# Two graph layers on one core: moving the feature loads and stores to the Scalar engine's queue, reordering the first three chunks and splitting the last row's work

## The reference

```python
# layer 1
x_norm = layernorm(x, g_in, b_in)
logits = x_norm @ Wn + bn
gumbel = -log(-log(clip(u, EPS, 1)) + EPS)
y = hard(softmax(logits + gumbel)) + y_soft - y_soft     # straight-through
gate = y[:, 1]                                           # one number per node
view2 = (adj * gate[:, None] * gate[None, :]) @ x_norm
g = sigmoid(concat([x_norm, view2]) @ Wg + bg)
x1 = layernorm(x + layernorm(g * (x_norm @ W1 + b1) + (1 - g) * (view2 @ W2 + b2) + x, g_out, b_out))
# layer 2, on the Poincare ball: xt is the tangent image of x1 @ weight.T with the bias added
s = adj @ xt
h = proj(expmap0(proj(expmap0(s))), relu in the tangent space)   # norms, tanh, artanh per row
out = layernorm(x1 + h)
```

## Time and profile before

| | |
|---|---|
| median of three runs | 991.94 us |
| the three runs | 991.94, 4496.1, 988.4 us |
| profiled execution | 988.93 us |
| its span, first to last instruction | 987.1 us |
| mean granted clock of TensorE | 0.981 |

### The profile page before, as it was taken

The page is one execution under the profiler, slowest core; times in us unless marked ns, Lnnn a source line. Parts: engine busy times, 40 slices in busy tenths (PEclk is TensorE's granted clock), DMA queues, the critical chain, the costliest instruction groups (busy, mean ns, idle before and its releaser), DMA issues.

```text
span 987.1 us, 12612 instructions
## 1 busy us (share of the span) xinstructions
PE 914.8 (93%) x4052; PEld 725.5 (73%) x4052; DVE 798.6 (81%) x1778; ACT 692.0 (70%) x1233; POOL 225.5 (23%) x201
## 2 busy tenths in 40 slices
PE   3897998999999999999999999998999988989992
PEld 2554776877787777888888888886778766768772
DVE  3567898988898889788685867769999986988984
ACT  4685686868676656856564664576988977887883
POOL 2220211111111111101110100102003627264562
PEclk8999999999999999999999999999999999999997
DMA  6888696876868586958584565757899988999970
GB/s 241 288 305 305 228 423 265 317 297 256 321 233 341 212 327 232 335 214 298 206 304 169 210 253 185 259 204 261 328 355 410 368 342 332 355 390 353 357 314 21
DMA packets 51681, 281.72 MB, mean 285 GB/s; under 512 B 6512, under 2 KB 8224, under 8 KB 20512
## 3 DMA queue, kind: packets, MB, share of 16 engines
q1 hardware_dynamic: 49888, 277.78, 75.1%
q10 hardware_dynamic: 1728, 3.15, 0.8%
HBM read 271.44 MB, written 9.46 MB: 285 GB/s over the span
## 4 chain that ended last, share of the span: by engine, by line
PE 48%; DVE 22%; POOL 12%; ACT 7%; issue 4%; DMA 4%; SPq 2%; POOLq 0%; DVEq 0%; ACTq 0%
PE PS L986 14%; PE PS L988 14%; PE PS L987 13%; DVE AL L741 6%; DVE XGL L741 4%; DVE XTL L741 2%; POOL SINV L485 2%; DVE BS L690 2%; PE PS L1075 2%; PE PS L1071 2%; DMA A<-in_adjT_dram 2%; POOL e_rc L492 1%; POOL r_rs L462 1%; PE PS L984 1%; DMA xnt_scratch<-XNT 1%
## 5 line engine op out<-in xcount | busy, mean ns | idle before, releaser
L741 DVE TENSOR_TENSOR AL<-A,AH 128x1024 fp32r<-128x1024 f32 x251 | 299.6, 1220 | 42.9 <-ACT AH L559 41.9
L559 ACT ACTIVATE AH<-A 128x1024 fp32r<-128x1024 f32 x251 | 256.3, 1057 | 103.2 <-PE PS L988 84.3
L741 DVE TENSOR_TENSOR XGL<-A,XGH 128x1024 fp32r<-128x1024 f32 x119 | 139.4, 1217 | 9.0 <-ACT XGH L559 8.8
L986 PE MATMUL PS<-AH,XGH 128*128 128x512 f32 x344 | 137.5, 400 | 5.6 <-DVE AL L741 5.6
L988 PE MATMUL PS<-AH,XGL 128*128 128x512 f32 x344 | 134.4, 391 | 0.0
L987 PE MATMUL PS<-AL,XGH 128*128 128x512 f32 x344 | 134.3, 390 | 0.0
L986 PE MATMUL PS<-AH,XTH 128*128 128x512 f32 x298 | 118.5, 398 | 6.4 <-DVE AL L741 6.3
L559 ACT ACTIVATE XGH<-A 128x1024 fp32r<-128x1024 f32 x119 | 117.8, 1054 | 2.1 <-DMA A<-in_adjT_dram 2.1
L987 PE MATMUL PS<-AL,XTH 128*128 128x512 f32 x298 | 117.4, 394 | 0.0
L988 PE MATMUL PS<-AH,XTL 128*128 128x512 f32 x298 | 117.3, 394 | 0.0
L741 DVE TENSOR_TENSOR XTL<-A,XTH 128x1024 fp32r<-128x1024 f32 x92 | 109.7, 1220 | 5.1 <-ACT XTH L559 4.7
(11 more groups left out here) (236 smaller groups left out, 1558.4 us busy)
## 6 DMA issues: line engine op xcount, KB each, us to landing
A<-in_adjT_dram SPq DMA_DIRECT2D x243, 1024.0 KB, 6.8
XR<-in_x_dram SPq DMA_DIRECT2D x16, 256.0 KB, 4.8
GB<-gate_scratch SPq DMA_DIRECT2D x12, 256.0 KB, 3.7
XNT<-xnt_scratch SPq DMA_DIRECT2D x12, 256.0 KB, 4.1
x_scratch<-X SPq DMA_DIRECT2D x12, 256.0 KB, 7.7
xnt_scratch<-XNT SPq DMA_DIRECT2D x6, 256.0 KB, 3.4
xnt_scratch<-X1T SPq DMA_DIRECT2D x6, 256.0 KB, 3.7
FU<-in_x_dram SPq DMA_DIRECT2D x4, 256.0 KB, 3.9
```

Of the source, the lines that this page charges most:

```text
L559: a.activation(high(m), A[:, n % RING, h * HW:(h + 1) * HW], ACT.Copy).then_inc(S["hi"], 1)
L741: v.tensor_tensor(low(m), A[:, n % RING, h * HW:(h + 1) * HW], high(m).bitcast(F32), ALU.subtract).then_inc(S["lo"], 1)
L986: p.matmul(acc, hi[:, st], high(m)[:, mv], start=start, stop=False)
```

## The change

1. **Queues.** `load_x` and `store_xnt` move from SP's stream to ACT's. ACT's stream begins with `load_x(0)` to `load_x(2)`; later loads stand behind `normalize`, stores behind `gated`. SP starts with U and BNB, then the norm vectors and A's first tile, and issues the A tiles in a plain loop.
2. **The first three chunks.** On DVE `stats_pre(0)` goes ahead of the first operation on U, `neg_mean_pre(0)` ahead of the second, and `gate_end(0)` ahead of `neg_mean_pre(2)`. On ACT each logarithm stands around `normalize(0)`, `transposed(0)` goes ahead of `normalize(1)`, an exponential of one column (JUNK) is added ahead of `store_xnt(0)`, and `normalize(2)` stands behind `gated(0)`. TensorE does `rows_and_logits(0)` ahead of `transposes(1)`.
3. **The last row** (o = 11). ACT leaves out the four squares ahead of the relu, and DVE gets those sums from `bn_stats` as 128 * (mean^2 + variance). POOL's power of eight columns becomes two of four, the relu's half first. The final scaling and shifting is done by ACT for the left half and DVE for the right, and each half has a store of its own.
4. **All rows:** the places of `norm` and `store` in ACT's order go from 21 and 22 to 22 and 23.

```diff
...
 DVE_SECOND = {"take": 3, "floor": 7, "norms": 11, "add": 15, "mean": 18}
-ACT_SECOND = {"relu": 7, "tanh": 14, "norm": 21, "store": 22}
+ACT_SECOND = {"relu": 7, "tanh": 14, "norm": 22, "store": 23}
 PE_SECOND = {"turn": 2}
...
         def _(sp):
-            def load_x(k):
-                if k >= 3:
-                    sp.wait_ge(S["pre_y"], k - 2)
-                sp.dma_start(XIN[k % 3][:, :], x[k * P:(k + 1) * P, :]).then_inc(S[f"xin{k % 3}"], 16)
-
-            def store_xnt(k):
-                sp.wait_ge(S["pre_xt"], k + 1)
-                sp.dma_start(xnt_dram[k * P:(k + 1) * P, :], XNTB[k % 2][:, :]).then_inc(S[f"xnt_stored{k % 2}"], 16)
-
             def load_a(n):
...
 
-            load_x(0)
+            sp.dma_start(U[:, :], u).then_inc(S["urow"], 16)
+            sp.dma_start(BNB[:, :], bn.partition_broadcast(P)).then_inc(S["urow"], 16)
             for t, v in ((GINC, g_in), (BINC, b_in)):
                 sp.dma_start(t[:, :], v.rearrange("(p o) -> p o", o=1)).then_inc(S["norm_vecs"], 16)
-            sp.dma_start(U[:, :], u).then_inc(S["urow"], 16)
-            sp.dma_start(BNB[:, :], bn.partition_broadcast(P)).then_inc(S["urow"], 16)
             sp.dma_start(IW[:, P:P + 2], wn).then_inc(S["norm_vecs"], 16)
-            load_x(1)
-            load_x(2)
             load_a(0)
...
                 sp.dma_start(t, v).then_inc(S["weights"], 16)
-            load_a(1)
-            load_x(3)
-            load_a(2)
-            load_x(4)
-            load_a(3)
-            store_xnt(0)
-            store_xnt(1)
-            for n in range(4, NCH):
-                store_xnt(n - 2)
-                if n + 1 < NCH:
-                    load_x(n + 1)
+            for n in range(1, NCH + 3):
                 load_a(n)
-            for k in range(NCH - 2, NCH):
-                store_xnt(k)
-                load_a(k + 2)
-            load_a(NCH + 2)
             for n in range(NCH + 3, NT):
...
             for i in range(4):
-                sp.wait_ge(S[f"res_stored{i}"], 16 * NCH // 4)
+                sp.wait_ge(S[f"res_stored{i}"], 16 * (NCH // 4 + (i == 3)))
 
...
                 if event == "floor" and o >= ON_DVE_FROM:
-                    pow_half("s2max", o + 1 - ON_DVE_FROM, sinv, sr, "s2inv")
+                    pow_half("s2max", 1, sinv[:, BLK:], sr[:, BLK:], "s2inv")
+                    pow_half("s2max", 2, sinv[:, 0:BLK], sr[:, 0:BLK], "s2inv")
                 if event == "floor" and o < ON_DVE_FROM:
...
 
-            act.wait_ge(S["gum1"], 1)
-            a.activation(U[:, :], U[:, :], ACT.Ln).then_inc(S["gum2"], 1)
-            act.wait_ge(S["gum1"], 2)
-            a.activation(U[:, :], U[:, :], ACT.Ln).then_inc(S["gum2"], 1)
+            def load_x(k):
+                wait_n(act, "pre_y", k - 2)
+                act.dma_start(XIN[k % 3][:, :], x[k * P:(k + 1) * P, :]).then_inc(S[f"xin{k % 3}"], 16)
+
+            def store_xnt(k):
+                act.wait_ge(S["pre_xt"], k + 1)
+                act.dma_start(xnt_dram[k * P:(k + 1) * P, :], XNTB[k % 2][:, :]).then_inc(S[f"xnt_stored{k % 2}"], 16)
+
+            for k in range(3):
+                load_x(k)
+
+            def gumbel_ln(i):
+                act.wait_ge(S["gum1"], i + 1)
+                a.activation(U[:, :], U[:, :], ACT.Ln).then_inc(S["gum2"], 1)
 
...
 
+            gumbel_ln(0)
             normalize(0)
+            gumbel_ln(1)
+            load_x(3)
+            transposed(0)
+            act.wait_ge(S["const"], 1)
+            a.activation(JUNK[:, 0:1], NHALF[:, 0:1], ACT.Exp)
+            store_xnt(0)
             normalize(1)
-            transposed(0)
-            normalize(2)
             gate_exp(0)
+            load_x(4)
             transposed(1)
             gated(0)
+            store_xnt(1)
+            normalize(2)
             gate_exp(1)
+            load_x(5)
             for k in range(NCH):
...
                     gated(k + 1)
+                if k + 2 < NCH:
+                    store_xnt(k + 2)
                 if k + 3 < NCH:
...
                 gated_high(k)
+                if k + 6 < NCH:
+                    load_x(k + 6)
                 if k + 2 < NCH:
...
                     a.activation(RELU[i][:, :], E[:, i, :], ACT.Relu).then_inc(S["relu"], 1)
-                    for t in range(BLK):
+                    for t in range(BLK if o < NCH - 1 else 0):
                         a.activation(JUNK[:, blk(t)], E[:, i, blk(t)], ACT.Square, accum_out=SR[:, i, t:t + 1])
...
                     act.wait_ge(S["nm3"], o + 1)
-                    for t in range(BLK):
+                    for t in range(BLK if o < NCH - 1 else BLK // 2):
                         last = a.activation(RESULT[o % 4][:, blk(t)], RESULT[o % 4][:, blk(t)], ACT.Identity,
...
                     c = ROWS[o]
+                    left = slice(0, CW if o < NCH - 1 else CW // 2)
                     act.wait_ge(S["res"], o + 1)
-                    act.dma_start(out[c * P:(c + 1) * P, :], RESULT[o % 4][:, :]).then_inc(S[f"res_stored{o % 4}"], 16)
+                    act.dma_start(out[c * P:(c + 1) * P, left], RESULT[o % 4][:, left]).then_inc(S[f"res_stored{o % 4}"], 16)
+                    if o == NCH - 1:
+                        act.wait_ge(S["res_right"], 1)
+                        act.dma_start(out[c * P:(c + 1) * P, CW // 2:], RESULT[o % 4][:, CW // 2:]).then_inc(S["res_stored3"], 16)
 
...
             link = Link(dve, S["dve_link"])
-
-            dve.wait_ge(S["urow"], 32)
-            v.tensor_scalar(U[:, :], U[:, :], U_EPS, 1.0, ALU.max, ALU.min).then_inc(S["gum1"], 1)
 
...
             stats_pre(0)
+            dve.wait_ge(S["urow"], 32)
+            v.tensor_scalar(U[:, :], U[:, :], U_EPS, 1.0, ALU.max, ALU.min).then_inc(S["gum1"], 1)
+            neg_mean_pre(0)
             dve.wait_ge(S["gum2"], 1)
...
             stats_pre(1)
-            neg_mean_pre(0)
+            neg_mean_pre(1)
             dve.wait_ge(S["gum2"], 2)
...
                                    op0=ALU.mult, op1=ALU.add).then_inc(S["gumbel"], 1)
-            stats_pre(2)
-            neg_mean_pre(1)
             dve.wait_ge(S["gumbel"], 1)
             gate_begin(0)
+            stats_pre(2)
+            gate_end(0)
             neg_mean_pre(2)
-            gate_end(0)
             stats_pre(3)
...
                 if event == "floor" and o >= ON_DVE_FROM:
+                    dve.wait_ge(S["relu"], o + 1)
+                    for t in range(BLK):
+                        last = v.bn_stats(BS[:, t, :], E[:, i, blk(t)])
+                    link(last)
+                    dve.nop(nofuse=True)
+                    for t in range(BLK):
+                        last = v.bn_aggr(MV3[:, i, t, :], BS[:, t, :])
+                    link(last)
                     dve.wait_ge(S["sq3"], o + 1)
-                    v.tensor_scalar(SR[:, i, :], SR[:, i, :], MIN_NORM2, None, ALU.max).then_inc(S["s2max"], 1)
+                    v.tensor_scalar(SR[:, i, BLK:], SR[:, i, BLK:], MIN_NORM2, None, ALU.max).then_inc(S["s2max"], 1)
+                    link(v.tensor_tensor(e["v"], MV3[:, i, :, 0], MV3[:, i, :, 0], ALU.mult))
+                    link(v.tensor_tensor(e["v"], e["v"], MV3[:, i, :, 1], ALU.add))
+                    v.tensor_scalar(SR[:, i, 0:BLK], e["v"], float(P), MIN_NORM2, ALU.mult, ALU.max).then_inc(S["s2max"], 1)
                 if event == "norms" and o >= ON_DVE_FROM:
-                    dve.wait_ge(S["s2inv"], o + 1 - ON_DVE_FROM)
-                    v.tensor_scalar(e["w"], SINV[:, i, 0:BLK], ATANH_MAX_NORM, 1.0, ALU.mult, ALU.min)
+                    dve.wait_ge(S["s2inv"], 1)
                     link(v.tensor_tensor(e["nr"], SINV[:, i, BLK:], SR[:, i, BLK:], ALU.mult))
+                    dve.wait_ge(S["s2inv"], 2)
+                    link(v.tensor_scalar(e["w"], SINV[:, i, 0:BLK], ATANH_MAX_NORM, 1.0, ALU.mult, ALU.min))
                     link(v.tensor_tensor(e["nr"], e["nr"], e["w"], ALU.mult))
...
                     neg_mean(MV3[:, i, :, :], e["rs"], e["nm"], "nm3")
+                    if o == NCH - 1:
+                        dve.wait_ge(S["nm3"], NCH)
+                        for t in range(BLK // 2, BLK):
+                            last = v.tensor_scalar(RESULT[o % 4][:, blk(t)], RESULT[o % 4][:, blk(t)], e["rs"][:, t:t + 1],
+                                                   e["nm"][:, t:t + 1], ALU.mult, ALU.add)
+                        last.then_inc(S["res_right"], 1)
 
...
             transposes(0)
+            rows_and_logits(0)
             transposes(1)
-            rows_and_logits(0)
             rows_and_logits(1)
...
```

2 lines of the change are left out of this document (1 added, 1 removed).

## The result

| | before | after |
|---|---|---|
| median of five runs | 991.75 us | 979.39 us |
| lowest and highest | 988.4, 4496.1 us | 977.9, 981.38 us |
| profiled execution | 988.93 us | 979.39 us |
| its span | 987.1 us | 977.6 us |
| mean granted clock | 0.981 | 0.986 |

The ratio is 0.9888, with a 95% interval from 0.9864 to 0.9911: 1.1% less, within the 2% called no change here. (Three executions of this study, one of before and two of queue_undo, took 2376 to 4496 us and are part of no ratio.) The forecast was 978.3 us. The profiled executions differ by 9.54 us, where the sum had 10.6.

What follows compares the result with a forecast made beforehand. TensorE, 93% busy, was taken as the bound, so savings had to come where it starts late or has ended: 7.7 (start) + 0.5 (norm) + 2.4 (tail) = 10.6 us off 988.93 gives 978.3, range 973 to 987.

Steps and rivals of the forecast that it cites:

- the sum: Whole kernel: start 7.7, norm 0.5 and tail 2.4 make 10.6 us saved, from 988.93 to 978.3.
- First term: Start: with the new order of the first chunks, transposes(2) starts at 18.6 instead of 21.36, 2.75 us.
- Second and third term: Chunk 2: TensorE's gap from 25.62 to 28.93 goes, 3.3 us; clock stays high, 1.65 us (0 to 3.2).
- The start as a whole: Start: 2.75 + 3.3 + 1.65 = 7.7 us, handed on whole through the storing of the gates.
- The median has room: Chunk loop: a store has 8.5 us to land; ACT-queue result stores had median 5.8, longest 9.0.
- The rival of late landings: Chunk loop: landings over 8.5 us hold transposed five times; at 11.83, 16.7 us lost, 994.4; chance 0.07.
- What the move costs ACT: Chunk loop: 24 DMA issues join ACT's stream, covered by its backlog, cost nothing; uncovered 8.2 us.
- The rival of 984.5: Chunk loop: ACT pays 0.34 us for each load and store issue, giving 984.5; chance 0.13.
- The norm's place: All rows: norm one split later in ACT's order shortens waits, 0 to 1.8 us, taken as 0.5.
- The last row: Tail: earlier relu, split sums and powers, and halved norm save 2.4 us, bounds 0.7 and 2.6.
- The power beside DVE's multiply: Last row: POOL's first power might take 1.85 us instead of 1.02; were both so, only 0.3 left.
- the 1.95 of relu, sums and powers: Last row: relu starts at 971.1, DVE makes four sums, powers ready at 975.5 instead of 977.46, 1.95 us.

Runs made afterwards that it cites:

- queue_undo: The kernel after with x loads and stores of XNT put back into SP's queue in the order of before; 987.74 us, ratio 0.9961.
- places_undo: The kernel after with the places of norm and store put back to 21 and 22; 982.49 us, ratio 0.9922.
- last_undo: The kernel after with the last row's sums, powers, norm and store as before, new places kept; 981.60 us, ratio 0.9912.
- last_sums_undo: The kernel after with only the last row's sums and powers as before, halved norm and two stores kept; 983.62 us in a single run.
- a_held: The kernel after with A tile n, from 2 on, issued only when chunk n is transposed; 983.90 us, ratio 0.9935.
- loads_undo: The kernel after with only the x loads put back into SP's queue, stores of XNT still in ACT's; 983.09 us, ratio 0.9932.
- issues_double: The kernel after with each x load and each store of XNT issued as two halves; 986.66 us, ratio 0.9963.
- a_held_early: The kernel after with only A tiles 2 to 8 held, tile n until chunk n is transposed; 980.53 us, ratio 0.9904.

## Why the prediction held, and where it did not

**First term (2.75 us, the order).** Right: 21.36 - 18.46 = 2.90. What it left unsaid is that it is worth nothing by itself; queue_undo had it in full and had the gates no earlier.

**Second and third term (3.3 and 1.65, the stall and the clock).** Right: from `transposes(2)` to the logits of chunk 2 are 3.90 us for 7.57, 3.67 less, and from there to the next transposes 2.61 for 4.25, 1.64 less. Together with the first term 8.2, at chunk 3. The third is in part luck. When TensorE gets to the high level differs between executions of the same program: in after during the first half tile (3.16 us), in places_undo, last_undo and last_sums_undo only behind it (3.62), with logits of 1.92, 1.80 and 1.11 us. There the third term came to 0.8, 0.9 and 1.6 us, inside its bounds of 0 and 3.2, and chunk 3's transposes 6.9 to 7.8 us ahead of before.

**The start as a whole (7.7).** Mis-sized: 5.5 at the gates, 4.9 to 5.1 in the three other kernels with the same start. The step that failed is "tiles 1 to 4 are issued at once; the loop doesn't wait for A now, and that earns nothing by itself". It asked only whether someone waits for A, not what the tiles do to the other transfers. The windows show the engines full from 20 to 40 us, and the landings in ACT's queue went up to 10.7 us with a median near 6 over the run; among those issued between 15 and 45 us the median was 8.1 for loads and 8.3 for stores. "The median has room" was read from result stores of the whole run, and this stretch was not like them. The rival of late landings named the place and the point, 10.6 us, but only for stores, at five pairs of rounds. In the runs it was x's loads that ended last, in two rounds, and it cost 2.1 us; with a fourth buffer for x the stores took their place (11.07 us) and 1.7 of the 2.1 stayed. That rival's 994.4 is also a slip: 978.3 + 16.7 = 995.0.

The Trainium skill, "DMA: Bandwidth & Descriptors", section "Issuing engines are not separate DMA queues", had been weighed against this edit. Its rule, that all issuers share the same engines, is what a_held shows: with less in SP's queue the landings in ACT's queue cease to hold the rounds. Its consequence, that a second issuer saves issue time only, holds better than the prediction took it. Of the 9.9 us by which the first store of XNT is there sooner than in queue_undo, 6.3 are its earlier issue and the rest the shorter landing (8.3 for 12.0); for x's chunk 3, against loads_undo, 4.1 are the issue and 0.7 the landing. But that issue time is not the small thing that the section calls it: an issue took 0.3 to 0.4 us, and what counted was the place behind loads, stores and A tiles in SP's order. The landing of 8.3 was longer than the median of 5.8 that the second term went by; at 18.7 us it was still in time for the 19.9 of `transposed(2)`.

**What the move costs ACT (nothing).** Right at one issue per cover, with the limit that issues_double shows. The rival of 984.5 falls: rounds without a DMA wait have the old 5.1.

**The norm's place (0.5 in the middle, between 0 and 1.8).** The size was right: 0.7, in TensorE's waits ahead of row 10's and row 11's transposes. The whole middle can't show it, since it scatters by up to 4. The rows behind the estimate were misread, though. Between 765 and 965 us ACT waits seven times ahead of a norm, not eight, and the stall of 1.76 us at 845.58 is gone in after and in places_undo alike, so it was not the place's; that the estimate came out is luck.

**The last row (2.4).** Right within 0.2. In the working the place was inside the 1.95 of relu, sums and powers; the runs part it as 1.60 and 0.42 (2.02 together), and the half norm with its second store as 0.55 for 0.45. The power beside DVE's multiply, feared at 1.85, was not: two took 1.98.

**The sum.** 10.6 against 9.54: 2.2 less in the start at the gates, of which 0.6 came back by GB (less than the 0.9 by which this stretch scatters), 0.3 more in the middle and 0.2 more in the tail.

## What to carry to other kernels

A wait in a shared queue also meters what stands behind it. Here it kept the A tiles back, and with it gone they filled the DMA engines. Take the waiting transfer out, and ask what the rest of the queue will now do to everybody's transfers; look at the DMA share of exactly that stretch, and take landing times from rows beside equally full engines. Split a transfer's delay into the time until its issue and the time from issue to landing, before you say what another queue gives it. Two edits to one chain can be worth more together than apart (here 5.5 us for 2.9 and nothing): price each with the other in place. A reordering that frees an engine pays only when the thing waited for next is there. And when the whole scatters by more than the effect, look for the one wait that the edit should change, over all kernels that have it.

## What the hardware showed besides

**The gates' way through memory varies.** The same store of the gates took 4.62 us to land in after, 7.31 in a_held_early and 9.60 in a_held. In a_held the ring was being filled just then (DMA share 1.01 and 1.02 from 70 to 80 us, at 413 and 431 GB/s). In a_held_early it was not (0.86 from 75 to 80 us, where after has 0.91), and loads_undo, with no hold and 0.77 from 80 us on, had 6.07; what makes those two late is open. In a_held_early a gain of 2.4 us ahead of this store shrank to 1.3 behind it.

**Durations and the clock row can disagree.** In after the granted clock of the stretch from 19 to 21 us is 1.00, the 2.4 GHz level, while the first half tile in it took 3.16 us, and the same four matmuls take 1.88 from 23.25 on. In before the row has 0.50 there. Windows of both kernels:

```profile
19.00:21.00 2.00, 2.00 (x5) 1.04 (x4) 1.11 (x10) 0.94 (x2) 1.01 (x1) 1.00 1.00 415
```

```profile
19.00:21.00 2.00, 1.53 (x7) 1.54 (x8) 0.81 (x5) 1.43 (x5) 0.00 (x0) 0.50 1.03 424
```

So at the start I read the level from the durations.

**The middle breathes by some microseconds.** In every kernel the granted clock is at 0.50 in a few spells of 2 to 8 us behind idle stretches of TensorE (3.11 us until 792.64 in after, for instance), near 92, 168, 680, 798, 836 and 888 us, and which of them occur differs from trace to trace: worked out from windows of 2 us, 13.6 us in all in before, 13.7 in after, 10.2 in queue_undo, 22.8 in a_held. The longest middle belongs to the last, but the order of the others does not follow the spells exactly, so the link is likely and not shown. It needs no edit: last_sums_undo, whose middle is after's, has 20.5 us of such spells and a middle 2.9 longer, and five executions of after itself lie between 977.9 and 981.4 us. A change of one or two microseconds in the chunk loop, seen at the gates, can't be found again in the whole.
